# Tokens first in each turn of the slot loops, and the last tile of attention ahead of the router's choice

## What is computed

```python
x = x + 0.5 * ffn(layernorm(x))
x = x + attn(layernorm(x))
x = x + 0.5 * ffn(layernorm(x))

def ffn(x):                       # 16 experts, 4 of them per token
    shared = (silu(x @ G.T) * (x @ U.T)) @ D.T * sigmoid(x @ sgate.T)
    weights, ids = top_k(softmax(x @ gate_w.T), 4)
    for e in range(16):
        coef = sum(where(ids == e, weights, 0))
        acc += (silu_and_mul(x @ w13[e].T) @ w2[e].T) * coef
    return shared + acc

def attn(x):                      # gated linear attention, 2 heads, a chunked scan
    q, f, v = silu(x @ Wq.T), sigmoid(x @ Wk.T), x @ Wv.T
    o = chunked_gla(q, v, log_sigmoid(f))
    return rmsnorm(o, w) @ Wo.T
```

## Time and profile before

| | us |
|---|---|
| median of 3 runs | 512.98 |
| lowest, highest | 512.23, 513.92 |
| profiled execution, its time | 512.58 |
| profiled execution, its span | 510.8 |
| PE busy | 424.4 (83% of the span) |
| DVE busy | 302.5 (59%) |
| ACT busy | 203.0 (40%) |
| POOL busy | 192.0 (38%) |

### The profile page before, as it was taken

The page is one execution under the profiler, slowest core; times in us unless marked ns, Lnnn a source line. Parts: engine busy times, 40 slices in busy tenths (PEclk is TensorE's granted clock), DMA queues, the critical chain, the costliest instruction groups (busy, mean ns, idle before and its releaser), DMA issues.

```text
span 510.8 us, 8760 instructions
## 1 busy us (share of the span) xinstructions
PE 424.4 (83%) x2241; PEld 328.5 (64%) x2245; DVE 302.5 (59%) x943; ACT 203.0 (40%) x564; POOL 192.0 (38%) x207
## 2 busy tenths in 40 slices
PE   6976199699999999979979877417999999999980
PEld 4433065499999988534679643304569999998750
DVE  5750288756666665395786563104766666666447
ACT  3320065356666655215656420000115666565500
POOL 0277600024444445450254037750003444444553
PEclk9997589789999999998989979577999999999995
DMA  7999443034444432830000195322003444443282
GB/s 268 295 342 393 150 131 94 2 90 135 134 139 134 133 122 71 302 124 0 0 1 1 43 373 188 120 100 69 2 0 110 134 133 132 135 132 116 73 337 81
DMA packets 41023, 68.17 MB, mean 133 GB/s; under 512 B 5072, under 2 KB 32208, under 8 KB 40976
## 3 DMA queue, kind: packets, MB, share of 16 engines
q1 hardware_dynamic: 33392, 45.84, 28.8%
q0 software_dynamic: 7584, 21.77, 12.0%
HBM read 42.42 MB, written 25.17 MB: 132 GB/s over the span
## 4 chain that ended last, share of the span: by engine, by line
PE 70%; DVE 13%; another core or an unknown queue 7%; issue 5%; ACT 3%; DMA 1%; DVEq 0%
PE ps L422 8%; PE ps L476 7%; PE ps L445 7%; PE ps L472 6%; PE ps L473 6%; PE ps L427 5%; PE ps L457 4%; PE ps L564 3%; PE ps L500 2%; PE ps L504 2%; PE ps L505 2%; PE ps L502 2%; PE ps L501 2%; PE ps L483 2%
## 5 line engine op out<-in xcount | busy, mean ns | idle before, releaser
L900 POOL DMA_INDIRECT rows<-ar,idx x94 | 90.3, 960 | 192.1 <-ACT ar L750 191.5
L445 PE MATMUL ps<-WS,ar 128*128 128x256 f32 (+1 forms) x192 | 52.9, 426 | 43.4 <-DVE ar L994 18.8
L893 POOL DMA_INDIRECT slots<-XR,pos x64 | 61.7, 964 | 59.7 <-DVE pos L1079 36.7
L445 PEld LDWEIGHTS ps<-WS,ar 128*128 128x128 f32 (+1 forms) x192 | 39.9, 213 | 61.1 <-issue 23.8
L1122 DVE SCALAR_TENSOR_TENSOR ar<-ps,XR,ar 128x112 f32<-128x112 f32 x94 | 31.4, 334 | 65.0 <-ACT ar L744 61.7
L472 PE MATMUL ps<-WH,xt 128*128 x188 | 63.0, 336 | 5.7 <-DVE WL L1018 3.5
L733 ACT ACTIVATE ar<-ps 128x512 f32<-128x512 f32 (+1 forms) x24 | 14.3, 596 | 127.8 <-remote 71.7
L473 PE MATMUL ps<-WL,xt 128*128 x188 | 62.1, 331 | 0.0
L744 ACT ACTIVATE ar<-ps 128x176 f32<-128x176 f32 x94 | 29.9, 318 | 70.5 <-issue 44.5
L422 PE MATMUL ps<-XT,WS 128*128 128x512 f32 x96 | 51.7, 666 | 1.0 <-ACT sgt L727 1.0
L476 PE MATMUL ps<-WH,xl 128*128 x188 | 50.9, 353 | 0.3 <-DVE xl L1138 0.3
(11 more groups left out here) (167 smaller groups left out, 863.4 us busy)
## 6 DMA issues: line engine op xcount, KB each, us to landing
XR<-slots SPq DMA_DIRECT2D x94, 144.0 KB
WR<-w SPq DMA_DIRECT2D x8, 1408.0 KB
WR<-rows SPq DMA_DIRECT2D x16, 512.0 KB, 7.8
slots<-zeros SPq DMA_DIRECT2D x1, 2304.0 KB, 12.3
MR<-w2r SPq DMA_DIRECT2D x2, 1024.0 KB
MR<-w2m SPq DMA_DIRECT2D x1, 1792.0 KB, 10.0
rows<-ar,idx POOLq DMA_INDIRECT x94
X<-x SPq DMA_DIRECT2D x4, 256.0 KB, 4.4
```

What stands on the lines that cost most here:

```text
L445: mm = pe.matmul(ps[:, 2 * h + i // 2, i % 2 * D:(i % 2 + 1) * D], Hs[u % 2][rows, tok(i)], WS2[rows, j, :], start=first and i % 2 == 0, s ...
L893: pool.indirect_dma_start(out=slots_dram[:, :], out_offset=bass.IndirectOffsetOnAxis(ap=pos[:, t, r:r + 1], axis=0), in_=XR[:, t, :], in_o ...
L900: pool.indirect_dma_start(out=rows_dram[:, :], out_offset=bass.IndirectOffsetOnAxis(ap=idx[:, i:i + 1], axis=0), in_=ys[i % NY], in_offset ...
```

## The change

It has three pieces.

**Tokens first.** In both slot loops PE's `slot_turn(f, i + 1)` stands ahead of `slot_in(f, i)`, ACT's `turned(i + 1)` ahead of `silu(i)`, and DVE's `left(i + 1)` ahead of `hidden(i)`.

**The last tile ahead of the choice.** `choose` is split into `judge` (maximum and difference) and `choose` (the rest). At the end of attention `scale(2, 7)` comes first, then `judge(1, 0)`, `choose(1, 0)`, `judge(1, 1)` and `places(1, 0)`; ACT's `router(1, 0)` comes behind the copy of the last tile. In the first layer the order of these stays.

**Ranks behind the first unit.** PE's `ranks(1, 0)` moves from the end of attention to behind `unit_in(1, 0)`, as it was in the first layer already. Two of the five groups of three warm matmuls at the end of attention go.

```diff
@@ tensor, ffn
                 unit_in(f, 0)
+                ranks(f, 0)
                 if f == 0:
-                    ranks(0, 0)
@@ tensor, ffn
                 for i in range(TL + 2):
+                    if i + 1 < TL:
+                        slot_turn(f, i + 1)
                     if i < TL:
                         slot_in(f, i, e[i])
                     if i + 1 < TL and len(e) == i + 1:
                         e.extend(experts_from(i + 1, mybir.EngineType.PE))
-                    if i + 1 < TL:
-                        slot_turn(f, i + 1)
@@ tensor, attention
                         logits(1, i - 6)
-                    if i == NT + 4:
-                        ranks(1, 0)
-                    if i >= NT + 1:
+                    if NT < i < NT + 4:
 
                         keep_warm(3, B_KV)
@@ scalar, slots
                 for i in range(TL + 2):
+                    if i + 1 < TL:
+                        turned(i + 1)
                     if i < TL:
                         silu(i)
-                    if i + 1 < TL:
-                        turned(i + 1)
@@ scalar, attention
                 for i in range(3, NT + 5):
                     step(i)
-                    if i == NT + 3:
-                        router(1, 0)
+                router(1, 0)
@@ vector, choose
-            def choose(f, h):
+            def judge(f, h):
                 some = half_tiles(h)
                 dve.wait_ge(s_lg, 2 * f + h + 1)
                 logit = logits_of(h)[:, :, 0:NE]
                 link(dve.tensor_reduce(t1[:, some], logit, AX.X, ALU.max))
                 dve.tensor_tensor(lg[:, some, :], logit, experts(t1[:, some]), ALU.subtract).then_inc(s_lgc, 1)
+
+            def choose(f, h):
+                some = half_tiles(h)
                 dve.wait_ge(s_ex, 2 * f + h + 1)
@@ vector, slots
                 for i in range(TL + 1):
-                    if i < TL:
-                        hidden(i, e[i])
                     if i + 1 < TL:
                         if len(e) == i + 1:
                             e.extend(experts_from(i + 1, mybir.EngineType.DVE))
                         left(i + 1)
+                    if i < TL:
+                        hidden(i, e[i])
@@ vector, ffn
             def ffn(f):
+                if f == 0:
+                    judge(f, 1)
                 choose(f, 1)
@@ vector, attention
                         scale(2, i - 4)
-                    if i == NT + 2:
-                        choose(1, 0)
+                judge(1, 0)
+                choose(1, 0)
+                judge(1, 1)
                 places(1, 0)
@@ vector, the program's start
             dve.wait_ge(s_cst, 16)
+            judge(0, 0)
             choose(0, 0)
```

## The result

The changed kernel takes 492.6 us in the median of four runs (489.97 to 496.45), beside 513.45 for the kernel before on the same chip: ratio 0.959, 95% interval 0.951 to 0.967. A second set of runs, on another chip, gave 494.97 and a ratio of 0.966 (0.963 to 0.969).

The account below looks back on a forecast made before the run. Bound: a 2.06 us ring around a PE needing 2.00 in the slot loops, and PE signals seen late during dispatch. Savings 3.0 + 3.8 + 0.6 + 4.4 = 11.8 us gave 501.0 us, range 495.5 to 507.

Parts of the forecast that it names:

- Part 1, loops: Both slot loops: tokens-first order saves 3.8 us in the first and 3.0 in the second, bounds 2.0 to 8.5.
- the ring: Slot loops: Silu, `hidden`, next `xl` and L476 wait on each other for 2.06 us; PE needs 2.00.
- load turns: Slot-loop turns loading eight expert numbers: 2.43 us before; 2.2 us extra per loop kept in the forecast.
- The fronts: First turns of the slot loops: 0.8 us gained in the first loop, 0.2 lost in the second.
- Part 2, the way to the dispatch: End of attention, second layer: POOL's first dispatch 0.6 us earlier; at half clock up to 2.4 us lost.
- Part 3, the late signals: Second layer, dispatch to `unit_out(3)`: earlier ranks get PE's signals out before the delay, 4.4 us saved, bounds 0 to 9.5.
- early tables: Rival, second layer's dispatch: tables get through early, that stage gives 8 to 9.5 us, total 496.5; chance 14%.
- The rule that was weighed: Dispatch: DVE and POOL share ports under an exclusive lock, so DVE is free only after POOL; late-signals gain would be nothing.
- Turns of 2.06: Rival, slot loops: another ring of that length appears, loops give 2.0 us, total 505.8; chance 8%.
- only the fronts: Rival: only the loops' fronts gain, neither turns nor dispatch, total 510 to 512 us; chance 4%.
- Signals hold until POOL is done: Rival, second layer's dispatch: signals arrive only after POOL ends, stage gives 0 to 2 us, total 504.4; chance 16%.
- Late rows: Rival, slot loops: slow tile loads stop PE each turn, 535 us; chance 3%, shared with half clock without other gains.

Follow-up runs that it names:

- e4: Kernel before with only ACT's copy of tile i + 1 ahead of Silu and DVE's `xl` ahead of `hidden`, PE's order as before; ratio 0.985.
- e2: Changed kernel with the three order edits of the slot loops undone, leaving the changed end of attention and ranks; ratio 0.983.
- v4: Changed kernel with a 128-column memset and a wait behind each dispatch transfer in both layers, one every 1.46 us; 464.8 us, ratio 0.903.
- v6: Changed kernel, both layers, first half's 16 dispatch transfers spaced at 1.46 us, second half's set for 1.36 us; 460.2 us, ratio 0.894.
- second trace: Profiled execution of the unchanged repeat of the changed kernel, run as a control on another chip; median 494.97 us, ratio 0.966.
- v1: Changed kernel with POOL holding the second half's 16 dispatch transfers until the tables are made, in both layers; 459.1 us, ratio 0.894.
- e9: Changed kernel with a memset and a wait behind each of the second layer's 32 dispatch transfers, one every 1.59 us; ratio 0.946.
- e8: Kernel before with POOL holding the second half's 16 dispatch transfers of the second layer until the tables are made; ratio 0.963.
- e3: Kernel before with only PE's transposition of tile i + 1 ahead of tile i's matmuls, ACT and DVE as before; ratio 1.001.

## Why the forecast was wrong, point by point

**Part 1, loops: right in the mechanism, wrong in the size.** Forecast 6.8, measured 12.0, outside the bounds of 2.0 to 8.5. The usual turn (2.00 forecast, 2.01 measured) and the ring were right. What was mis-sized is what I kept beside it. The step that failed is the load turns: I left 2.2 us in each loop because a load "holds PE's queue behind L476 as before", a price read in a loop where PE's queue was never ahead; some 0.3 is left of the 4.4 (4.1 us). My upper bound had the loads hidden, but 8.5 is the 6.8 and only one loop's 1.7. The fronts were the second term: `slot_out` has no work in the first two turns and `slot_hidden` none in the first, so these take 1.2 and 1.6 us in the second loop, once the ring is open, where I priced 2.00 and charged 0.2 more (1.4), the last turn takes 1.87 in both (0.3), and the first loop's front gives 1.4 instead of 0.8 (0.6). The usual turn of 2.013 instead of 2.00 takes back 1.1. Together that is 5.3, and 5.2 are missing. With its usual turns of 2.00 and load turns near 2.35, what I had in fact priced was close to ACT's and DVE's order alone: e4's 6.6 us.

**Part 2, the way to the dispatch: right at full clock, but the clock was lower.** 0.6 us earlier was forecast, and at full clock it is about that (102.1 to 102.5 for 102.8 to 103.4); `scale(2, 7)` then starts 93.5 to 93.9 us behind the last L472 of the first loop (e2, v4, v6), with 93.2 forecast. In the profiled execution the dispatch was 3.0 us later against the end of the first loop, 0.6 beyond the bound of 2.4, and in the second trace 3.5. I had tied half clock to the warm matmuls taken out; it fell ahead of them, behind a wait of 1.12 us that the kernel before has as well, and there the clock stayed high (L645 at 287.30 lasts 1.10 us). `scale(2, 7)` was forecast at 291.7 and started at 288.16, which is 294.7 on the scale of before once the 6.6 us of the first loop are added back.

**Part 3, the late signals: direction right, size too small.** Forecast 4.4, bounds 0 to 9.5; measured 8.0 at `unit_out(3)` in the first trace, and 6.4 at the loop, since that unit then ran at half clock (3.47 us instead of 1.89). In the second trace it was 13.7 and 10.7, beyond the upper bound. The step that failed is to take the first layer as the nearest row: it has the same delay itself (L1107 16.7 us behind the end of L408, 14.2 to 18.5 in the other traces without a pause or spacing there; L1107 then runs 22.8 us behind the first transfer with a pause, in v1, instead of 39.6), and the delay is no fixed price: the runs fit a backlog that depends on how many transfers are ahead of a signal. L408 was 28.4 us behind the first dispatch before, 18.5 and 16.2 in the two traces after, and DVE saw it 15.9, 14.3 and 9.4 us behind its end. The second thing missed is that ACT is held too: the Silu of unit 3 started 21.1 and 17.5 us behind the end of its matmuls in the two traces, and `unit_out(3)` followed it. I had named the earlier ranks as the reason for "early tables" but gave it 14%. That the stage gave 10.7 us in one execution and 6.4 in another is not explained by any run.

**The rule that was weighed** was rightly left out. In e9 DVE runs the first row of tables in the middle of the dispatch, 0.9 us behind the start of L408. As I had read the exclusive lock of which the Trainium skill speaks, page "SBUF — State Buffer", section "SBUF: two separate sides", DVE would have had to wait until POOL is done. My reading was too wide: the section ties the lock to DVE operations in a 2-port mode or with two SBUF inputs, and lets it go with each instruction. L1107 has a single input, in PSUM, so e9 speaks against my reading and not against the page. Nor would the lock explain that ACT is held, since by that section ACT never waits.

**The rivals.** "Early tables" (496.5) was the nearest to what happened in the stage; with the loops' 12 us it gives 491. "Turns of 2.06" and "only the fronts" are out. "Signals hold until POOL is done" is out for the tables (33.3 us, with POOL busy to 42.3), though not for ACT: the late Silu started at 339.34 and POOL's last transfer at 339.00; in the second trace it started 36.1 us behind the first transfer, with POOL busy to 42.5. "Late rows" are out: PE waits nowhere for a tile's rows in either loop of the changed kernel, busy 91.30 of 91.30 us in the second.

## What to carry to other kernels

When a ring in a pipelined loop is opened, price the turn by the bound engine's work alone, and look again at everything that cost something only because that engine's queue was never ahead: register loads, fronts without a last stage. A wait without a named releaser is worth an experiment before it is priced. Here one wait on POOL's queue, to hold back half of its indirect transfers, gave 14 us in one layer and 36 in both, the latter more than the whole change.

## What the runs showed of the hardware

- While POOL issues indirect transfers back to back (0.96 us each, one every 1.27 us), the signals of PE's matmuls reach DVE and ACT late, from some 11 us after the first transfer on: L408 by up to 18.5 us at DVE (e8, first layer), L422 by 21.1 us at ACT (the changed kernel, second layer) and by 22.3 in e3's first layer. DVE's signals are held too: by 2.5 us on the way to DVE itself (L1101 to L1102) and by 1.9 on the way to PE (L994 to L445), both before. At one transfer in 1.36 us the delay starts at 21 to 29 us and is at most 11.5; at 1.46 us or more there is none. The profile shows it as "remote", "issue" or a named releaser, with the row of the matmul long ended. The Trainium skill, page "Perfetto Trace Analysis", section "Tensor Engine Instruction (MATMUL, LD_WEIGHTS)", says why the row doesn't show it: a matmul's end in the profile is estimated from its size and the SBUF delay, and the semaphore update is pushed and spread after that, outside the profiled window. The runs agree: L408 has the same 0.83 us in the first layer of v1, where DVE sees it 0.6 us behind its end, and of the changed kernel, where it takes 15.9 us.
- A load of eight numbers into PE's registers (0.6 to 0.8 us) costs some 0.33 us of a 2 us turn when PE's queue is 0.3 us ahead of the array (e4), and nothing when it is 1.2 us ahead. One that took 1.28 us still cost 0.1 to 0.2.
- Matmuls of the same shape took 1.10 us at the higher and 1.96 us at the lower level of PE's clock, and the same wait of 1.12 us ahead of them was followed by either level in different executions.
- Of 1216 indirect transfers of the dispatch, in 19 traces, 76 took over 1.2 us instead of 0.96, and each of these overlaps a series of DVE's weight subtractions, whose two inputs lie in SBUF.
